# Ternarising the FFN weights inside the first supertile instead of in a stage of their own

## What is computed

```python
def weight_quant(w):
    scale = 1.0 / jnp.clip(jnp.mean(jnp.abs(w)), EPS)
    wq = jnp.clip(jnp.round(w * scale), -1.0, 1.0) / scale
...
gate = bitlinear(x, w_gate)          # w_gate, w_up: (8192, 2048)
up = bitlinear(x, w_up)
intermediate = silu(gate) * up
return h_bitlinear(intermediate, w_down)   # Hadamard transform first; w_down: (2048, 8192)
```

## Time and profile before

| | us |
|---|---|
| time, median of 2 runs | 14870.67 (14851.64 to 14889.7) |
| the profiled execution's own time | 14634.0 |
| its span, slowest core | 14632.2 |
| spans of the 8 cores | 14486.3 to 14632.2 |

### The profile page before, as it was taken

The page is one execution under the profiler, slowest core; times in us unless marked ns, Lnnn a source line. Parts: engine busy times, 40 slices in busy tenths (PEclk is TensorE's granted clock), DMA queues, the critical chain, the costliest instruction groups (busy, mean ns, idle before and its releaser), DMA issues.

```text
span 14632.2 us, 81285 instructions; the slowest of 8 cores (14486.3 to 14632.2 us)
## 1 busy us (share of the span) xinstructions
PE 5329.0 (36%) x23765; PEld 2324.0 (16%) x23765; DVE 4479.0 (31%) x7927; ACT 1361.4 (9%) x2661; POOL 133.6 (1%) x135
## 2 busy tenths in 40 slices
PE   1555244445436510000000002923680567067506
PEld 0222112212112200000000000311230223023202
DVE  3111211111230043223333332265128323822571
ACT  2000211111110122220000000100110011001000
POOL 0000000000000000000000000000000000000000
PEclk9777566666667755555555556866895789589857
DMA  1111111101012214774444445512560355045304
GB/s 48 16 15 15 51 12 10 13 9 13 12 33 40 29 52 135 220 222 119 124 125 124 125 125 120 114 37 51 124 130 7 85 120 107 0 109 127 76 6 121
DMA packets 2105923, 1104.21 MB, mean 75 GB/s; under 512 B 1761429, under 2 KB 1892502, under 8 KB 2093206
## 3 DMA queue, kind: packets, MB, share of 16 engines
q1 hardware_dynamic: 1874328, 1040.30, 28.7%
q0 software_dynamic: 231168, 58.73, 4.1%
HBM read 1006.65 MB, written 151.00 MB: 79 GB/s over the span
## 4 chain that ended last, share of the span: by engine, by line
PE 36%; DMA 24%; DVE 21%; issue 11%; ACT 6%; DVEq 1%; SPq 1%; POOL 0%; ACTq 0%; POOLq 0%
PE PA L58 25%; DVE ta L58 8%; PE PB L58 7%; DVE A L58 4%; DMA fbuf<-wup_bc 3%; DMA fbuf<-wgate_bc 3%; DMA fbuf<-wdown_bc 3%; PE PT L58 3%; ACT A L58 2%; ACT ta L58 2%; DVE cols L58 2%; DVE wsb L58 2%; DMA xt<-wgate_bc 2%; DMA xt<-wdown_bc 2%; DMA xt<-wup_bc 2%
## 5 line engine op out<-in xcount | busy, mean ns | idle before, releaser
L58 PE MATMUL PA<-A,wsb 128*128 128x512 bf16 x15360 | 3654.4, 401 | 1849.6 <-DMA wsb<-ternd_s 687.3
L58 PEld LDWEIGHTS PA<-A,wsb 128*128 128x128 bf16 x15360 | 1548.7, 102 | 3924.6 <-issue 2455.2
L58 PE MATMUL PT<-consts,colb 128*1 128x128 bf16 x87 | 23.0, 265 | 2915.5 <-DVE colb L58 2915.5
L58 PE MATMUL PB<-A,wsb 128*128 128x512 bf16 x4096 | 934.9, 388 | 138.3 <-ACT A L58 101.9
L58 DVE TENSOR_REDUCE cols<-xt 128x1 f32<-128x2048 f32 x144 | 329.2, 2286 | 1045.3 <-DMA xt<-wgate_bc 240.3
L58 DVE TENSOR_SCALAR ta<-ta,cols 128x512 f32<-128x512 f32 (+1 forms) x768 | 581.0, 756 | 83.8 <-DVE ta L58 1.8
L58 DVE SCALAR_TENSOR_TENSOR A<-A 128x512 bf16<-128x512 bf16 x768 | 531.8, 692 | 82.3 <-DVE A L58 3.2
L58 PEld LDWEIGHTS PB<-A,wsb 128*128 128x128 bf16 x4096 | 398.3, 99 | 673.8 <-issue 277.3
L58 DVE TENSOR_SCALAR ktmb<-PT,cols 128x128 bf16<-128x128 bf16 x512 | 145.3, 284 | 1105.8 <-PE PT L58 1105.8
L58 DVE TENSOR_TENSOR ssb<-PS,mh 128x128 bf16<-128x128 f32 x256 | 74.6, 291 | 1317.1 <-PE PS L58 1317.1
L58 PE MATMUL PT<-consts,sb 128*128 128x128 bf16 x272 | 29.9, 227 | 1219.1 <-DVE sb L58 1212.6
(11 more groups left out here) (113 smaller groups left out, 4585.2 us busy)
## 6 DMA issues: line engine op xcount, KB each, us to landing
wsb<-terng_s SPq DMA_DIRECT2D x256, 512.0 KB, 4.5
wsb<-ternu_s SPq DMA_DIRECT2D x256, 512.0 KB, 6.4
xt<-x_own SPq DMA_DIRECT2D x32, 1024.0 KB
terng_s<-wsb SPq DMA_DIRECT2D x64, 512.0 KB, 4.0
ternu_s<-wsb SPq DMA_DIRECT2D x64, 512.0 KB, 4.0
ternd_s<-wsb SPq DMA_DIRECT2D x64, 512.0 KB, 4.0
xt<-x_pref SPq DMA_DIRECT2D x16, 1024.0 KB
wsb<-wk_bc POOLq DMA_DIRECT2D x32, 512.0 KB, 6.4
```

The costliest lines, as they stand in the source:

```text
L58: inst = getattr(eng, method)(**kwargs)
```

## The change

The ternary stage and its barrier are taken out. The 192 blocks are made ternary inside supertile 0, each just before it is first used, by a new function `tern_inline`; supertiles 1 to 3 read the ternary scratch in HBM as before, and so does supertile 0.

- In iteration `jo` of the gate and up loop of supertile 0, `tern_inline` is called for the gate block (`par` 0) and the up block (`par` 1), ahead of the loads `wgd` and `wud`. These then wait for the stores (`dq3`, `dq4`).
- In the down loop of supertile 0, `tern_down_col(fo + 1)` makes four blocks ternary (`par` 0, 1, 0, 1) between the two groups of 32 matmuls of column `fo`, ahead of `dn_load(fo + 1, 0)`, which waits for the stores.
- Every `tern_inline` loads its block into one buffer, `Sst`. The load waits for all VectorE and ScalarE work emitted so far.
- A block is worked on in two halves of 1024 columns. With `par` 1, VectorE does three `tensor_scalar` instructions on each half, as before. With `par` 0, ScalarE computes sign(scale w - 0.5) and sign(scale w + 0.5) and VectorE adds the two. Both give twice the ternary value; the factor 0.5 is put into the weight scales `CO_MW` with one small instruction.
- The outputs go to `qh` and `kh` and are stored from there.

The diff, without the lists of semaphores, to which `dq5` and `dq6` are added, and without the body of the removed `tern_block` loops where it says nothing new:

```diff
         CO_ACC = 352
+        CO_HP = 348
+        CO_HN = 349
...
+        r.emit("vector", "memset", dict(ap=c_(CO_HP), constant=0.5))
+        r.emit("vector", "memset", dict(ap=c_(CO_HN), constant=-0.5))
...
+        vm2 = r.emit("vector", "tensor_scalar",
+                     dict(out=cols[:, CO_MW:CO_MW + 3], in0=cols[:, CO_MW:CO_MW + 3],
+                          scalar1=0.5, scalar2=None, op0=ALU.mult), waits=[("sv", vm2)])
...
+        tern_g_done = {}
+        tern_u_done = {}
+        tern_d_done = {}
-        def tern_block(src, dst, ws_idx, i, width=None):
-            wd = D if width is None else width
-            par = i % 2
-            qs = "dq" if par == 0 else "dq2"
+        tn_store3 = [0]
+        tn_store4 = [0]
+
+        def tern_inline(src_ap, dst_ap, ws_idx, par, key, width=D):
             ss = "dq3" if par == 0 else "dq4"
-            stage = xt[:, 0:wd] if par == 0 else fbuf[:, 0:wd]
-            oslot = wsb[:, 0:wd] if par == 0 else wsb[:, 2048:2048 + wd]
+            oslot = qh[:, 0:width] if par == 0 else kh[:, 0:width]
             d_ = r.emit("sync", "dma_start",
-                        dict(out=stage.rearrange("p (k c) -> p k c", c=128), in_=src),
-                        waits=([tn_cons[i - 2]] if (i - 2) in tn_cons else
-                               [("sv", r.val("sv")), ("sa", r.val("sa"))]),
-                        inc=(qs, 16))
-            v_ = r.emit("vector", "tensor_scalar",
-                        dict(out=ta[:, 0:wd], in0=stage, scalar1=c_(CO_WS + ws_idx),
-                             scalar2=c_(CO_A), op0=ALU.mult, op1=ALU.add),
-                        waits=[(qs, d_), ("sv", r.val("sv"))])
-            tn_cons[i] = ("sv", v_)
-            v_ = r.emit("vector", "tensor_scalar",
-                        dict(out=ta[:, 0:wd], in0=ta[:, 0:wd], scalar1=c_(CO_A), scalar2=1.0,
-                             op0=ALU.subtract, op1=ALU.min), waits=[("sv", v_)])
-            v_ = r.emit("vector", "tensor_scalar",
-                        dict(out=oslot, in0=ta[:, 0:wd], scalar1=-1.0, scalar2=None,
-                             op0=ALU.max),
-                        waits=[("sv", v_), (ss, tn_store.get(i - 2, 0))])
-            tn_store[i] = r.emit("sync", "dma_start",
-                                 dict(out=dst, in_=oslot.rearrange("p (k c) -> p k c", c=128)),
-                                 waits=[("sv", v_)], inc=(ss, 16))
-
-        ti = 0
-        for i in range(IC):
-            tern_block(wgate_bc[i].rearrange("(k p) c -> p k c", p=128),
-                       terng_s[i].rearrange("(k p) c -> p k c", p=128), 0, ti)
-            ti += 1
-        for i in range(IC):
-            tern_block(wup_bc[i].rearrange("(k p) c -> p k c", p=128),
-                       ternu_s[i].rearrange("(k p) c -> p k c", p=128), 1, ti)
-            ti += 1
-        for i in range(FC * 4):
-            col, piece = i // 4, i % 4
-            tern_block(wdown_bc[col][piece * (I // 4):(piece + 1) * (I // 4)]
-                       .rearrange("(k p) c -> p k c", p=128),
-                       ternd_s[col][piece * (I // 4):(piece + 1) * (I // 4)]
-                       .rearrange("(k p) c -> p k c", p=128), 2, ti, width=I // 4)
-            ti += 1
-        barrier()
+                        dict(out=Sst[:, 0:width].rearrange("p (k c) -> p k c", c=128),
+                             in_=src_ap),
+                        waits=[("sv", r.val("sv")), ("sa", r.val("sa"))],
+                        inc=("dq5", 16))
+            hw = width // 2
+            vlast = None
+            for hh in range(2):
+                sl = slice(hh * hw, (hh + 1) * hw)
+                if par == 0:
+                    s1 = r.emit("scalar", "activation",
+                                dict(out=xt[:, 0:hw], in_=Sst[:, sl], func=AF.Sign,
+                                     scale=c_(CO_WS + ws_idx), bias=c_(CO_HN)),
+                                waits=[("dq5", d_), ("sa", r.val("sa")),
+                                       ("sv", r.val("sv"))])
+                    s2 = r.emit("scalar", "activation",
+                                dict(out=xt[:, hw:2 * hw], in_=Sst[:, sl], func=AF.Sign,
+                                     scale=c_(CO_WS + ws_idx), bias=c_(CO_HP)),
+                                waits=[("sa", s1)])
+                    vlast = r.emit("vector", "tensor_tensor",
+                                   dict(out=oslot[:, sl], in0=xt[:, 0:hw],
+                                        in1=xt[:, hw:2 * hw], op=ALU.add),
+                                   waits=[("sa", s2), ("sv", r.val("sv")),
+                                          (ss, tn_store3[0])])
+                else:
+                    scr = ta[:, D - hw:D]
+                    v_ = r.emit("vector", "tensor_scalar",
+                                dict(out=scr, in0=Sst[:, sl], scalar1=c_(CO_WS + ws_idx),
+                                     scalar2=c_(CO_A), op0=ALU.mult, op1=ALU.add),
+                                waits=[("dq5", d_), ("sv", r.val("sv"))])
+                    v_ = r.emit("vector", "tensor_scalar",
+                                dict(out=scr, in0=scr, scalar1=c_(CO_A), scalar2=1.0,
+                                     op0=ALU.subtract, op1=ALU.min), waits=[("sv", v_)])
+                    vlast = r.emit("vector", "tensor_scalar",
+                                   dict(out=oslot[:, sl], in0=scr, scalar1=-1.0, scalar2=2.0,
+                                        op0=ALU.max, op1=ALU.mult),
+                                   waits=[("sv", v_), (ss, tn_store4[0])])
+            stc = r.emit("sync", "dma_start",
+                         dict(out=dst_ap, in_=oslot[:, 0:width]
+                              .rearrange("p (k c) -> p k c", c=128)),
+                         waits=[("sv", vlast)], inc=(ss, 16))
+            if par == 0:
+                tn_store3[0] = stc
+            else:
+                tn_store4[0] = stc
+            return stc
 
         SBG = fbuf[:, 0:G]
         SBU = fbuf[:, G:2 * G]
@@ -856,16 +871,25 @@
             for jo in range(IC):
                 par = jo % 2
                 qsem = "dq" if par == 0 else "dq2"
+                if s == 0:
+                    tern_g_done[jo] = tern_inline(
+                        wgate_bc[jo].rearrange("(k p) c -> p k c", p=128),
+                        terng_s[jo].rearrange("(k p) c -> p k c", p=128), 0, 0, jo)
+                    tern_u_done[jo] = tern_inline(
+                        wup_bc[jo].rearrange("(k p) c -> p k c", p=128),
+                        ternu_s[jo].rearrange("(k p) c -> p k c", p=128), 1, 1, jo)
                 wgd = r.emit("sync", "dma_start",
                              dict(out=wsb[:, par * 2 * D: par * 2 * D + D]
                                   .rearrange("p (k c) -> p k c", c=128),
                                   in_=terng_s[jo].rearrange("(k p) c -> p k c", p=128)),
-                             waits=([("sp", sp_mms.get(jo - 2, 0))] if jo >= 2 else []),
+                             waits=([("sp", sp_mms.get(jo - 2, 0))] if jo >= 2 else []) +
+                                   [("dq3", tern_g_done[jo])],
                              inc=(qsem, 16))
                 wud = r.emit("sync", "dma_start",
                              dict(out=wsb[:, par * 2 * D + D: par * 2 * D + 2 * D]
                                   .rearrange("p (k c) -> p k c", c=128),
                                   in_=ternu_s[jo].rearrange("(k p) c -> p k c", p=128)),
+                             waits=[("dq4", tern_u_done[jo])],
                              inc=(qsem, 16))
                 qtot = r.val(qsem)
                 PSG = PB[:, 0:G] if par == 0 else PA[:, 0:G]
@@ -1024,7 +1048,20 @@
                                       in_=sb512[:, 0:G].rearrange("p (t c) -> p t c", c=128)),
                                  waits=[("sa", sad)], inc=("dq3", 16))
 
-            dn_load(0, 0, [("sv", r.val("sv")), ("sg", r.val("sg")), ("sa", r.val("sa"))])
+            def tern_down_col(col):
+                for piece in range(4):
+                    stc = tern_inline(
+                        wdown_bc[col][piece * (I // 4):(piece + 1) * (I // 4)]
+                        .rearrange("(k p) c -> p k c", p=128),
+                        ternd_s[col][piece * (I // 4):(piece + 1) * (I // 4)]
+                        .rearrange("(k p) c -> p k c", p=128), 2, piece % 2, None,
+                        width=I // 4)
+                tern_d_done[col] = (tn_store3[0], tn_store4[0])
+
+            if s == 0:
+                tern_down_col(0)
+            dn_load(0, 0, [("sv", r.val("sv")), ("sg", r.val("sg")), ("sa", r.val("sa")),
+                           ("dq3", tern_d_done[0][0]), ("dq4", tern_d_done[0][1])])
             dn_load(0, 1, [])
             for fo in range(FC):
                 par = fo % 2
@@ -1042,7 +1079,11 @@
                            inc=(("sp", 1) if k == ICH - 1 else False))
                 dn_mid[fo] = r.val("sp")
```

(24 more changed lines are left out.)

## The result

| | before | after |
|---|---|---|
| median of the timed runs, us | 14708.48 (10 runs) | 15612.32 (11 runs) |
| ratio to before, 95% interval | | 1.0636 (1.0595 to 1.0676) |
| span of the profiled execution, slowest core | 14632.2 | 15674.0 |

The changed kernel is 6.4% slower, 0.0636 x 14708 = 935 us; the two medians differ by 904. The ratios in this document are of executions outside a slower state, some per cent longer, into which a program on all eight cores falls at times, and so are the traces, but for that of direct_and_ahead, which was taken in it. The prediction's +932 us on 14870.67 is +6.3%. Its time, 15800, lies 188 us above the measured one; most of that is the median of before, which over more runs is 162 us lower than the one that the prediction started from.

What follows compares the result with a forecast made beforehand. The old ternary stage was taken as bound by latency, the changed gate and up loop as one serial chain. +824 us there and +108 in the down loop made +932 on 14870.67, rounded to 15800 us, range 15500 to 16130.

Steps and rivals of the forecast that it cites:

- matmuls, `t8`, copy: Gate and up loop: 32 matmuls, `t8` and the ScalarE copy, 7.96 us plus 1.65 for idle TensorE, 9.6.
- gate load: Gate and up loop: load with nothing else in flight, 7.6 us from issue to first instruction, 7.7 with the handoff.
- gate computation: Gate and up loop: two halves of sign, sign, add at 3.7 us each, 7.4 us.
- period: Gate and up loop: seven links sum to 47.2 us an iteration, 64 make 3021 us, 824 more than before.
- No overlap in the gate and up loop: Each iteration's ternary work waits for the previous matmuls, and its own matmuls wait for it: one chain.
- The pointer operands: Gate and up loop: Sign's two pointer operands, about 93 ns each, would add 48 us; no row shows it.
- Sign and its table: Rival, gate and up loop: a table load before each Sign, 82 us more, 15885; chance 0.22.
- TensorE at its lower level: Rival, gate and up loop: each burst 13.7 instead of 8.7 us, 320 us more, 16120; chance 0.06.
- The down loop: Supertile 0: matmuls hidden beside the ternary chain, 72 us a column, 1173 us against 1065, 108 more.
- 7 us of queueing: Down loop, between columns: 2 MB ahead of the next column's first load, taken as 7 us, bounds 0 to 9.4.
- hidden matmuls: Rival, gate and up loop: matmuls hidden after all, 9.6 us less an iteration, 614 in all, 15190; chance 0.05.
- loads running ahead: Rival, both loops: fp32 loads landed before the previous computation ends, 1570 us off, 14230; chance 0.02.

Runs made afterwards that it cites:

- direct_and_ahead: Inline form with VectorE only, two buffers with loads issued once read, ternary blocks written straight into the matmuls' buffer, no reload in supertile 0; 0.8531 of before.
- early_gate_load: Changed kernel, but supertile 0's gate load waits only for the last reading of `Sst`, not all VectorE and ScalarE work; 1.0405 of before.
- down_load_first: Changed kernel, but in supertile 0's down loop the next column's first ternary load is issued ahead of the two matmul weight loads; 1.0537 of before.
- loads_ahead: vector_only with a buffer each for gate and up blocks, next iteration's two loads issued behind the up block's reload; 14109.26 us against 14772.99 before.
- vector_only: Changed kernel with the ScalarE branch taken out, every block going through VectorE's three instructions on each half; 1.0413 of before.
- keep_busy: Changed kernel with 150 added matmuls, result unread, behind each iteration's tail in supertile 0's gate and up loop; 1.0653 of before.
- keep_busy_longer: As keep_busy, but with 174 added matmuls in each iteration instead of 150; 1.0632 of before.
- stage_loads_ahead: Kernel before, separate ternary stage kept, each load issued once its buffer has been read, ahead of the previous block's store; 0.9069 of before.

## Why the prediction was right

The steps, with what the trace of after and the runs show:

| link of an iteration | predicted | measured in the timeline above |
|---|---|---|
| matmuls, `t8`, copy | 9.6 | 10.3 (7907.49 to 7917.74); bursts 9.09 us on the mean |
| gate load | 7.7 | 6.6 |
| gate computation | 7.4 | 8.2 |
| up load | 8.4 | 8.5 |
| up computation | 5.3 | 5.3 |
| landing of the up store | 4.5 | 4.3 |
| reload of up | 4.3 | 4.8 |
| period | 47.2 | 48.1 for this one, 47.67 (mean of 63) |

- **No overlap in the gate and up loop.** Right; the load follows the copy by 0.1 us, and early_gate_load shows that the wait is what puts it there.
- **Sizes.** Four terms were off by 0.5 to 1.1 us, three too small and one too large, and most of the errors cancel; that the period came within 0.5 us is in part luck. The load with nothing else in flight was taken from one row of the old stage, 7.6 us; here it takes 6.5, and no run says why. The gate computation was too short by 0.8: a straight line gave 1.06 us for a ScalarE instruction of 1024 columns, and it takes 1.24, as this group of the kernel after shows.

```profile
L58 ACT ACTIVATE xt<-Sst,cols 128x1024 f32<-128x1024 f32 x384 | 476.1, 1240 | 1497.8 <-DMA Sst<-wdown_bc 872.3 <-DMA Sst<-wgate_bc 456.8 <-DVE qh L58 150.8
```

- **The pointer operands.** The rows from which the line was drawn have no operand `cols`. The difference is 0.18 us an instruction. The Trainium skill, "ScalarE: Activation LUTs", section "What ACT_TABLE_LOAD costs", gives about 93 ns for each pointer operand, two of them 0.19; this trace agrees with it. The prediction had this figure in a sentence of its own and left it out of the sum; no run takes the operands away, and the function is another one too, so their share is inferred from two groups of rows.
- **Sign and its table.** The rival didn't come true. The kernel after has as many table loads as before; the first line is of before, the second of after:

```profile
L58 ACT ACT_TABLE_LOAD x14 | 18.0, 1283 | 126.7 <-DVE ta L58 77.7 <-PE PA L58 33.3 <-DVE cols L58 15.7
L58 ACT ACT_TABLE_LOAD x14 | 18.0, 1283 | 126.2 <-DVE ta L58 74.6 <-PE PA L58 35.7 <-DVE cols L58 15.9
```

- **TensorE at its lower level.** A burst starts with weight loads 0.43 us apart, and near its end they are 0.26 apart, as these rows of the burst at 7907.49 show; 9.09 us on the mean where 8.7 were taken and 13.7 would have been the rival. Right in kind, 0.4 us too small.

```profile
7907.87 0.15 PEld L58 LDWEIGHTS PB<-A,wsb 128*128 128x128 bf16 x1 [0.28 <-issue]
7908.30 0.15 PEld L58 LDWEIGHTS PB<-A,wsb 128*128 128x128 bf16 x1 [0.28 <-issue]
...
7915.05 0.11 PEld L58 LDWEIGHTS PB<-A,wsb 128*128 128x128 bf16 x1 [0.15 <-issue]
7915.31 0.11 PEld L58 LDWEIGHTS PB<-A,wsb 128*128 128x128 bf16 x1 [0.15 <-issue]
```

- **The down loop.** Predicted 72 us a column and +108 in all; from the first fp32 load of the first column (10178.5) to that of the last (11293.7) it is 74.3 us a column, and the windows give +145. The 2.3 us too few, 15 times, are 35 of the missing 37 us; 1.6 of them are the two gate-like computations of a column, short by 0.8 each as above. The terms between two columns, the landing, the issues and 7 us of queueing, sum to 13; down_load_first takes 193 us off, 13 for each of 15 columns. The 7 us had been a choice between 0 and 9.4, and no run measures them by themselves.
- **The sum** was +932 against 1002 by the windows of the profiled executions and 935 by the timed ratio. That 932 and 935 agree so closely is luck. The sum was built from rows of the profiled executions, and there the loops lost 70 us more. The prediction also took the timed median to lie 237 us above the profiled execution in both kernels; over all runs it is 74 above for before (14708 against 14634) and 63 below for after (15612 against 15675.6).
- **The two rivals that end faster or nearly so**, hidden matmuls and loads running ahead, were excluded by the order of the emitted waits, and not by any limit of the chip. loads_ahead and direct_and_ahead made the second one true. The prediction priced it too low: it reckoned with the two loads alone, 16.1 us an iteration and 1030 us in the gate and up loop. loads_ahead took 20.0 us off each iteration of vector_only, 1260 us, because the matmuls and the reload then left the chain as well, although the gate load stayed on it.

## What to carry to other kernels

Before moving work into a loop to hide it, follow the semaphores of one iteration: a wait for "everything so far" on the first load turns work that is beside into work that is behind, whatever the engines' busy shares say. The old ternary stage, with every engine and queue below half, was a chain of latencies, and the first remedy to try in such a case is to issue the loads earlier in place; here that alone gave 9%. The inline form paid as soon as its loads no longer waited for everything before them, 664 us less than before, and in full, 2170 us, once both loops had it so, the reload was gone and no load stood behind the landing of a store.

## What had not been expected of the hardware

- Some 6 us of idle ahead of a burst (5.65 to 7.11 in 16 bursts of keep_busy) cost as much as 38 us: 9.1 us on the mean in both. Idle stretches of 0.6 to 2.0 us (18 bursts of keep_busy_longer) cost nothing: 7.07 us in each. Nothing between was tried.
- With 174 added matmuls an iteration TensorE was busy 2833 of 2908 us and the granted clock was 1.00 over the loop, as the window of keep_busy_longer shows (columns as in the earlier trace rows). In the same loop of the kernel before, busy 518 of 579.5 us, the clock was 0.89 and many bursts took 8.56. The added matmuls multiply by an identity matrix; whether that is the reason was not tried.

```profile
6634.00:9542.00 2908.00, 2832.69 (x13073) 1274.68 (x13073) 564.09 (x693) 389.87 (x378) 0.00 (x0) 1.00 0.39 91
```

- In the gate and up loop of after one fp32 block of 1 MB was there 6.5 us after its issue with nothing else in flight, and some 8 us after it behind a store of 512 KB. With the queue kept full, in stage_loads_ahead, 1.5 MB passed every 5.75 us.
